# Sums over d of the first layer, moved from VectorE to ScalarE, in a fused interaction network

## The chip, the cores and the metric

One core of one Trainium2 chip runs the whole program. The metric is device microseconds of one execution, as the median of several. Times of instructions come from one profiled execution.

## The reference

For each of 2048 samples, 32 embedding rows of 16 numbers are gathered from 32 tables (x0: sample b, field m, dimension d). Three layers follow, each with 64 outputs k:

    xk = relu(einsum('bmd,bhd,mhk->bkd', x0, xk, W))
    outs.append(sum(xk, axis=d))

The first layer takes xk = x0 (32 rows h), the other two the 64 rows of the layer before. The 3 x 64 sums over d, joined with 16 dense features, go through an MLP of 208 to 512 to 256 to 1 with relu between. Everything is float32.

## The kernel before

**Tiling.** 64 samples make a turn; there are 32 turns (`STEPS`), indexed by s. Sample and d lie along the free dimension (1024 columns, `COLS`), and (m, h) pairs lie along the 128 partitions. A layer is a sum over chunks of 128 such pairs: the products x0[m] * xk[h] are made elementwise, and TensorE contracts them with the weights. Each chunk is contracted in two halves of 512 columns, half b into rows 64b to 64b+63 of a PSUM tile. The first layer (`layer0` in the code) has 5 chunks, since its products are symmetric; `layer1` and `layer2` (the second and third layer) have 16 each.

**Turn s** holds layer1(s) and layer2(s - 1), and in TensorE's queue layer0(s + 1) behind chunk 3 of layer2(s - 1). The MLP of 128 samples is spread over two turns: `mlp1` in even turns, `mlp2` and `mlp3` in odd ones. `mlp3` shares PSUM tile `acc0` with layer0.

**VectorE** makes 15 of the 16 product chunks of each of layer1 and layer2 in groups of 1 to 3 chunks, 7 from `xa` (plain copy of the layer's output, h rows twice) and 8 from `xb` (the same rows turned), both in PSUM. A ring of 10 chunks (`p_dve`) lies between it and TensorE. It also sums over d: `sums(s, n)` is one reduction of a 128 x 512 tile `out_l` into 32 columns per partition of `z`, one for each layer n in each turn. In a steady turn the queue holds: 3 groups of layer1 from xa; `sums(s, 0)`; `sums(s - 2, 1)`; 3 groups of layer1 from xb; `sums(s - 2, 2)`; 3 groups of layer2 from xa; 4 groups of layer2 from xb.

**GpSimd** gathers the table rows by indirect DMAs (16 a turn), makes the first layer's products from `q_tile` and one chunk (`p_pool`) of each other layer.

**ScalarE** evicts PSUM with relu. Its order in turn s is `x1_b(s)` (8 operations), `out_2(s - 2)`, `x2_a(s - 1)` (4 operations, allowed once VectorE is through with the xa groups of layer1(s)), `squares(s + 1)` (the first layer's fifth chunk, which waits for the DMA of `q_tile`), the eviction of mlp1 or mlp2, `x2_b(s - 1)` (8 operations, allowed once VectorE is through with the xb groups of layer1(s), and needed by the xb groups of layer2(s - 1)), mlp3's in odd turns, `x2_s` (the copy for GpSimd), `out_1`, in odd turns the moves of `z` into the MLP's input, then `x1_a(s + 1)`, `x1_s(s + 1)` and `out_0(s + 1)`, which writes the SBUF tile `out_l[:, 0]` that `sums(s + 1, 0)` reads. What is called plain x2 is `x2_a`.

**SyncE** loads the operand tiles (`spread`, `q_tile`) from a scratch tensor in device memory.

Of the kernel before, what the change touches and what calls it, by code (L numbers as in the profile page):

```python
# [7 lines left out]
ACT = mybir.ActivationFunctionType  # L8
# [6 lines left out]
DIM = 16  # L15
# [3 lines left out]
SB = 64  # L19
# [51 lines left out]
def dve_from(s, layer):  # L71


    if layer == 1:
        return max(0, 2 * CD * s - CD)
    return min(2 * CD * (s + 1), 2 * CD * STEPS - CD)
# [10 lines left out]
def build_kernel(nc, ids, table, first_row, dense_t, w0_mh, w0_hm, w1, w2, w_top1, b_top1, w_top2,  # L87
                 b_top2, w_top3, scratch, y):
    with ExitStack() as ctx:
        def sb(name, shape, dt=F32):  # L90
            return ctx.enter_context(nc.sbuf_tensor(name, shape, dt))
# [4 lines left out]
        def sem(name):  # L96
            return ctx.enter_context(nc.semaphore(name))
# [10 lines left out]
        out_l = sb("out_l", [P, 3, BLK])  # L108
        z = sb("z", [P, 2, 3, 2, SB // 2])
# [44 lines left out]
        out_ready = [sem(f"out{n}_ready") for n in range(3)]  # L154
        z_made = [sem(f"z{n}_made") for n in range(3)]
        z_moved = sem("z_moved")
# [146 lines left out]
        def _(act):  # L303
            def relu_a(acc, signal):

                for b in range(2):
                    for to in 0, K:
                        last = nc.scalar.activation(xa[to:to + K, b * BLK:(b + 1) * BLK],  # L308
                                                    acc[b * K:(b + 1) * K, :], ACT.Relu)
                last.then_inc(signal, 1)  # L310

            def relu_b(acc, signal):

                for b in range(2):
                    lo, hi = acc[b * K:b * K + FIELDS, :], acc[b * K + FIELDS:(b + 1) * K, :]
                    for q in range(Q):
                        last = nc.scalar.activation(  # L317
                            xb[q * FIELDS:(q + 1) * FIELDS, b * BLK:(b + 1) * BLK],
                            hi if q % 2 == 0 else lo, ACT.Relu)
                last.then_inc(signal, 1)  # L320
# [9 lines left out]
            def squares(s):  # L330

                act.wait_ge(q_loaded, 16 * Q * (s + 1))
                if s > 0:
                    act.wait_ge(l0_used, C0 * s)
                nc.scalar.activation(p_l0[0:FIELDS, CP, :], q_tile[0:FIELDS, :],  # L335
                                     ACT.Square).then_inc(squares_made, 1)
# [16 lines left out]
            def out_0(s):  # L353
# [2 lines left out]
                    act.wait_ge(z_made[0], s)  # L356
                nc.scalar.activation(out_l[:, 0, :], acc0[:], ACT.Relu).then_inc(out_ready[0], 1)

            def x1_b(s):

                if s == 1:
                    act.wait_ge(dve_made, CD)
                if s >= 2:
                    act.wait_ge(dve_made, dve_from(s - 2, 2) + CD)
                relu_b(acc0, x1b_ready)

            def x2_a(s):

                act.wait_ge(dve_used, dve_from(s, 1) + CD)
                if s + 1 < STEPS:  # L370
                    act.wait_ge(dve_made, dve_from(s + 1, 1) + POOL_CHUNK)
                else:
                    act.wait_ge(dve_made, dve_from(s - 1, 2) + POOL_CHUNK)
                relu_a(acc1[s % 2], x2a_ready)

            def x2_b(s):

                if s + 1 < STEPS:
                    act.wait_ge(dve_made, dve_from(s + 1, 1) + CD)
                else:  # L380
                    act.wait_ge(dve_made, dve_from(s - 1, 2) + CD)
                relu_b(acc1[s % 2], x2b_ready)
# [13 lines left out]
            def out_2(s):  # L396

                act.wait_ge(dve_used, dve_from(s, 2) + CD)
                if s > 0:
                    act.wait_ge(z_made[2], s)  # L400
                nc.scalar.activation(out_l[:, 2, :], acc2[:], ACT.Relu).then_inc(out_ready[2], 1)  # L401
# [24 lines left out]
            def mlp1(t):  # L426

                act.wait_ge(mlp_made, 3 * t + 1)
                for n in range(H1 // P):
                    last = nc.scalar.activation(h1[:, n, :], acc0[:, n * P:(n + 1) * P], ACT.Relu,  # L430
                                                bias=bt1[:, n:n + 1])
                last.then_inc(mlp_done, 1)
                if t + 1 < TILES:
                    load_dense(t + 1)

            def mlp2(t):

                act.wait_ge(mlp_made, 3 * t + 2)
                for n in range(H2 // P):
                    last = nc.scalar.activation(h2[:, n, :], acc0[:, n * P:(n + 1) * P], ACT.Relu,  # L440
                                                bias=bt2[:, n:n + 1])
                last.then_inc(mlp_done, 1)
# [16 lines left out]
            for s in range(STEPS):  # L459
                t = s // 2 - 2  # L460
                even = s % 2 == 0
                x1_b(s)
                if s >= 2:
                    out_2(s - 2)
                if s >= 1:
                    x2_a(s - 1)
                if s + 1 < STEPS:
                    squares(s + 1)
                if t >= 0 and even:
                    mlp1(t)  # L470
                if t >= 0 and not even:
                    mlp2(t)
                if s >= 1:
                    x2_b(s - 1)
                if t >= 0 and not even:
                    mlp3(t)
                if s >= 1:
                    x2_s(s - 1)
                    out_1(s - 1)
                if s % 2 == 1 and s >= 3:  # L480
                    move_z01(s // 2 - 1)
                    move_z2(s // 2 - 1)
                if s + 1 < STEPS:
                    x1_a(s + 1)
                    x1_s(s + 1)
                    out_0(s + 1)
# [17 lines left out]
        def _(dve):  # L504
# [33 lines left out]
            def sums(s, n):  # L538

                if s % 2 == 0 and s >= 4:  # L540
                    dve.wait_ge(z_moved, s // 2 - 1)
                dve.wait_ge(out_ready[n], s + 1)
                nc.vector.reduce_sum(z[:, s // 2 % 2, n, s % 2, :],  # L543
                                     out_l[:, n, :].rearrange("p (i d) -> p i d", d=DIM),
                                     AX_X).then_inc(z_made[n], 1)
# [26 lines left out]
            for s in range(STEPS):  # L572
                for c, n in GROUPS_L1:
                    if c == NT:
                        sums(s, 0)
                        if s >= 2:
                            sums(s - 2, 1)
                    if s == 0 and c == L0_OF_1_AFTER + 1:
                        first_layer_products(1)
                    layer1(s, c, n)  # L580
                if s >= 2:
                    sums(s - 2, 2)
                if s >= 1:
                    for c, n in GROUPS_L2:
                        layer2(s - 1, c, n)
# [178 lines left out]
```

## Time and profile before

| | |
|---|---|
| median of 3 runs | 1191.82 us (1191.45 to 1193.62) |
| profiled execution | 1192.97 us, span 1191.2 us |
| TensorE matmul busy | 1121.3 us (94%) |
| VectorE busy | 1118.8 us (94%) |
| GpSimd busy | 918.8 us (77%) |
| ScalarE busy | 733.9 us (62%) |
| mean granted TensorE clock | 0.991 of full speed |
| a steady turn | 34.62 us |

In rows of the timeline a line is a run of like instructions: start, duration of the whole run, engine, source line, what is written and read, and the count; in square brackets the idle time of the engine ahead of it and what ended it. A float32 matmul leaves two records in the trace, and so does its weight load, so 148 records of the layers are 74 matmuls, one turn's worth. A matmul record's end is modelled, so its pace is read from starts.

### The profile page before, as it was taken

The page shows a single profiled execution, that of the slowest core. Times are in us where ns is not written, and L with a number is a line of the kernel's source. Part 1 is how long each engine was busy: PE and PEld are TensorE (multiplying, and loading weights), DVE is VectorE, ACT ScalarE, POOL GpSimd, SP SyncE. Part 2 cuts the span into 40 slices and gives each one's busy share as a digit, 9 for nine tenths or more (in the row PEclk, how much of TensorE's full clock was granted, in tenths as well). Part 3 has the DMA queues.
Part 4 walks back from the last instruction along what each step waited for, and adds up shares of the span by engine and source line. Part 5 has one row for each costly group of instructions (what it writes and reads, how often), then busy time and mean ns, then how long its engine had stood idle before and what let it go on. Part 6 is the DMA issues. An engine that isn't in the chain of part 4 may idle for free.

```text
span 1191.2 us, 14658 instructions
## 1 busy us (share of the span) xinstructions
PE 1121.3 (94%) x5312; PEld 393.6 (33%) x5312; DVE 1118.8 (94%) x521; ACT 733.9 (62%) x1361; POOL 918.8 (77%) x640
## 2 busy tenths in 40 slices
PE   0488899999999999999999999999999999999997
PEld 0122223333333333333333333333333333333333
DVE  0487999999999999999999999999999999999995
ACT  0343666676667667665766766576676657657653
POOL 6688888888888888888888888888888888885400
PEclk9888999999999999999999999999999999999999
DMA  5887787667678766677876666788666778876300
GB/s 110 190 176 146 158 171 155 138 132 144 140 157 171 157 141 141 132 144 150 172 163 136 143 134 145 144 171 168 139 140 134 143 145 169 166 144 144 61 1 1
DMA packets 76216, 167.25 MB, mean 140 GB/s; under 512 B 21776, under 2 KB 39072, under 8 KB 76144
## 3 DMA queue, kind: packets, MB, share of 16 engines
q1 hardware_dynamic: 59216, 161.95, 64.8%
q0 software_dynamic: 16384, 4.23, 3.6%
q8 instruction: 42, 0.69, 0.3%
q10 hardware_dynamic: 544, 0.14, 0.1%
q14 instruction: 30, 0.25, 0.1%
HBM read 157.86 MB, written 8.40 MB: 140 GB/s over the span
## 4 chain that ended last, share of the span: by engine, by line
PE 86%; POOL 3%; DVE 3%; DMA 3%; issue 3%; ACT 1%; SPq 1%; DVEq 0%
PE acc L600 80%; POOL x_rows L254 3%; DVE p_dve L516 3%; PE acc L672 3%; PE acc L658 1%; PE acc L660 1%; DMA q_tile<-x_of_steps 1%; ACT xb L317 1%; DMA x_rows<-in_table,ids_s 1%; PE acc L680 1%; DMA spread<-x_of_steps 1%; SPq L192 1%; DMA x_of_steps<-x_rows 0%; SPq L219 0%; DVE z L543 0%
## 5 line engine op out<-in xcount | busy, mean ns | idle before, releaser
L600 PE MATMUL acc<-p_dve,w_s 128*64 128x512 f32 x3840 | 863.2, 598 | 22.5 <-DVE p_dve L516 21.8
L254 POOL DMA_INDIRECT x_rows<-in_table,ids_s x512 | 493.7, 964 | 146.1 <-issue 131.2
L516 DVE TENSOR_TENSOR p_dve<-spread,xb 128x3072 f32<-128x3072 f32 (+2 forms) x224 | 572.2, 2682 | 2.9 <-issue 2.9
L516 DVE TENSOR_TENSOR p_dve<-spread,xa 128x2048 f32<-128x2048 f32 (+1 forms) x192 | 501.5, 2730 | 16.6 <-issue 9.1
L600 PEld LDWEIGHTS acc<-p_dve,w_s 128*64 128x64 f32 x3840 | 267.9, 137 | 571.5 <-issue 467.2
L317 ACT ACTIVATE xb<-acc 32x512 f32<-32x512 f32 x512 | 288.8, 564 | 71.6 <-DVE p_dve L516 65.5
L266 POOL TENSOR_TENSOR p_l<-spread,q_tile 128x2048 f32<-128x2048 f32 x60 | 272.7, 4573 | 11.0 <-DMA q_tile<-x_of_steps 10.4
L308 ACT ACTIVATE xa<-acc 64x512 f32<-64x512 f32 x256 | 145.9, 570 | 189.6 <-PE acc L600 155.0
L277 POOL TENSOR_TENSOR p_pool<-spread,x_s 128x1024 f32<-128x1024 f32 x64 | 152.2, 2378 | 94.7 <-PE acc L600 45.9
L600 PE MATMUL acc<-p_l,w_s 128*64 128x512 f32 (+1 forms) x640 | 152.5, 612 | 41.6 <-DVE p_l L556 41.6
L326 ACT ACTIVATE x_s<-acc 64x512 f32<-64x512 f32 x256 | 151.5, 592 | 8.3 <-ACT y_row L449 4.8
L335 ACT ACTIVATE p_l<-q_tile 32x1024 f32<-32x1024 f32 x32 | 33.8, 1057 | 112.8 <-DMA q_tile<-x_of_steps 112.8
L600 PEld LDWEIGHTS acc<-p_l,w_s 128*64 128x64 f32 (+1 forms) x640 | 43.7, 139 | 144.9 <-issue 140.3
L543 DVE TENSOR_REDUCE z<-out_l 128x32 f32<-128x512 f32 x96 | 68.8, 776 | 4.5 <-ACT out_l L401 4.5
L600 PE MATMUL acc<-p_pool,w_s 128*64 128x512 f32 x256 | 65.8, 592 | 0.0
L672 PEld LDWEIGHTS acc<-h,wt 128*128 128x128 f32 x256 | 29.8, 191 | 13.6 <-issue 12.2
L672 PE MATMUL acc<-h,wt 128*128 128x128 f32 x256 | 32.8, 281 | 1.2 <-ACT h L430 1.2
L556 DVE TENSOR_TENSOR p_l<-spread,q_tile 128x2048 f32<-128x2048 f32 x4 | 9.2, 2291 | 25.8 <-DMA spread<-x_of_steps 25.8
L401 ACT ACTIVATE out_l<-acc 128x512 f32<-128x512 f32 x32 | 19.2, 600 | 19.4 <-PE acc L600 19.4
L600 PEld LDWEIGHTS acc<-p_pool,w_s 128*64 128x64 f32 x256 | 18.4, 137 | 36.5 <-issue 36.5
L658 PE MATMUL acc<-z_all,wt 128*128 128x128 f32 x128 | 26.4, 287 | 2.0 <-ACT z_all L407 2.0
L407 ACT ACTIVATE z_all<-z 64x64 f32<-64x64 f32 x96 | 24.3, 253 | 5.3 <-DVE z L543 4.1
(18 smaller groups left out, 151.1 us busy)
## 6 DMA issues: line engine op xcount, KB each, us to landing
spread<-x_of_steps SPq DMA_DIRECT2D x248, 512.0 KB, 17.4
q_tile<-x_of_steps SPq DMA_DIRECT2D x128, 128.0 KB, 11.4
x_rows<-in_table,ids_s POOLq DMA_INDIRECT x512
x_of_steps<-x_rows SPq DMA_DIRECT2D x64, 128.0 KB
spread<-x_of_steps SPq DMA_DIRECT2D x16, 256.0 KB, 5.4
w_s<-in_w SPq DMA_DIRECT2D x2, 512.0 KB, 5.7
wt<-in_w_top SPq DMA_DIRECT2D x1, 512.0 KB, 6.5
z_all<-in_dense_t ACTq DMA_DIRECT2D x16, 8.0 KB, 8.2
```

The lines of the kernel that those rows point to most:

```text
L254: nc.gpsimd.indirect_dma_start(out=x_rows[:, s % 2, i * DIM:(i + 1) * DIM], out_offset=None, in_=table, in_offset=bass.IndirectOffsetOnAxi ...
L266: nc.gpsimd.tensor_tensor(p_l0[:, c:c + 2, :], spread[:, s % 3, c:c + 2, :], q, ALU.mult).then_inc(l0_made, 2)
L277: nc.gpsimd.tensor_tensor(p_pool[:], spread[:, s % 3, POOL_CHUNK, :], x_s[:, layer - 1, :], ALU.mult).then_inc(pool_made, 1)
L308: last = nc.scalar.activation(xa[to:to + K, b * BLK:(b + 1) * BLK], acc[b * K:(b + 1) * K, :], ACT.Relu)
L317: last = nc.scalar.activation(xb[q * FIELDS:(q + 1) * FIELDS, b * BLK:(b + 1) * BLK], hi if q % 2 == 0 else lo, ACT.Relu)
L326: last = nc.scalar.activation(x_s[to:to + K, layer - 1, b * BLK:(b + 1) * BLK], acc[b * K:(b + 1) * K, :], ACT.Relu)
L335: nc.scalar.activation(p_l0[0:FIELDS, CP, :], q_tile[0:FIELDS, :], ACT.Square).then_inc(squares_made, 1)
L516: nc.vector.tensor_tensor(p_dve[:, to:to + n, :], spread[:, s % 3, tile:tile + n, :], over(x[:], n), ALU.mult).then_inc(dve_made, n)
L543: nc.vector.reduce_sum(z[:, s // 2 % 2, n, s % 2, :], out_l[:, n, :].rearrange("p (i d) -> p i d", d=DIM), AX_X).then_inc(z_made[n], 1)
L600: last = nc.tensor.matmul(acc[b * K:(b + 1) * K, :], w, prod[:, b * BLK:(b + 1) * BLK], start=start, stop=stop)
L658: nc.tensor.matmul(acc0[:, cols], wt1[:, 0, cols], z_all[:, 0, :], start=True, stop=False)
L672: last = nc.tensor.matmul(acc0[:, cols], wt2[:, k, cols], h1[:, k, :], start=(k == 0), stop=(k == H1 // P - 1))
```

## The change

`sums(s, 0)`, one VectorE reduction a turn, goes. In its place ScalarE makes the 32 sums of a turn by 32 activations of 128 x 16 columns each, in place on `out_l`, with relu (which changes nothing, since the tile has been through relu) and an accumulator output into one column of `z`. Sixteen of them stand behind `x2_a(s - 1)`, ahead of `squares(s + 1)`; sixteen behind the eviction of mlp1 or mlp2, ahead of `x2_b(s - 1)`. They do this in each turn from 0 on; in turn 0, where no x2_a is, both batches lie around `squares(1)`.

```diff
+            def sums_0(s, part):
+                act.wait_ge(out_ready[0], s + 1)
+                if part == 0 and s % 2 == 0 and s >= 4:
+                    act.wait_ge(z_moved, s // 2 - 1)
+                for i in range(part * SB // 4, (part + 1) * SB // 4):
+                    cols = out_l[:, 0, i * DIM:(i + 1) * DIM]
+                    last = nc.scalar.activation(cols, cols, ACT.Relu,
+                                                accum_out=z[:, s // 2 % 2, 0, s % 2, i:i + 1])
+                if part == 1:
+                    last.then_inc(z_made[0], 1)
...
                 if s >= 1:
                     x2_a(s - 1)
+                sums_0(s, 0)
                 if s + 1 < STEPS:
                     squares(s + 1)
                 if t >= 0 and even:
                     mlp1(t)
                 if t >= 0 and not even:
                     mlp2(t)
+                sums_0(s, 1)
                 if s >= 1:
                     x2_b(s - 1)
...
                     if c == NT:
-                        sums(s, 0)
                         if s >= 2:
                             sums(s - 2, 1)
```

## Rows read from the trace of the kernel before

**Rows 1.** The chain that ended last, two steady turns: start, duration, what.

```profile
548.82 32.38 PE acc L600 x148
581.20 1.98 PE acc L672 x16
583.18 7.02 PE acc L600 x32
590.73 25.34 PE acc L600 x116
618.05 32.39 PE acc L600 x148
```

**Rows 2.** Timeline of VectorE, one steady turn (s odd) and the next start.

```profile
569.99 7.83 DVE L516 TENSOR_TENSOR p_dve<-spread,xa 128x3072 f32<-128x3072 f32 x3
577.65 1.36 DVE L543 TENSOR_REDUCE z<-out_l 128x32 f32<-128x512 f32 x2
578.84 8.89 DVE L516 TENSOR_TENSOR p_dve<-spread,xb 128x3072 f32<-128x3072 f32 x3
587.56 0.77 DVE L543 TENSOR_REDUCE z<-out_l 128x32 f32<-128x512 f32 x1
588.16 7.83 DVE L516 TENSOR_TENSOR p_dve<-spread,xa 128x2048 f32<-128x2048 f32 x3
595.82 8.96 DVE L516 TENSOR_TENSOR p_dve<-spread,xb 128x3072 f32<-128x3072 f32 x4
604.61 7.83 DVE L516 TENSOR_TENSOR p_dve<-spread,xa 128x3072 f32<-128x3072 f32 x3
```

**Rows 3.** Timeline of TensorE's weight loads: steady pace, then a late chunk.

```profile
606.89 0.14 PEld L600 LDWEIGHTS acc<-p_dve,w_s 128*64 128x64 f32 x2 [0.29 <-issue]
...
615.04 0.14 PEld L600 LDWEIGHTS acc<-p_dve,w_s 128*64 128x64 f32 x2 [0.28 <-issue]
...
627.48 0.14 PEld L600 LDWEIGHTS acc<-p_dve,w_s 128*64 128x64 f32 x2 [0.29 <-issue]
628.46 0.20 PEld L600 LDWEIGHTS acc<-p_dve,w_s 128*64 128x64 f32 x4 [0.84 <-DVE p_dve L516]
628.94 0.14 PEld L600 LDWEIGHTS acc<-p_dve,w_s 128*64 128x64 f32 x2 [0.29 <-issue]
```

**Rows 4.** Timeline of ScalarE, the same odd turn.

```profile
577.92 2.31 ACT L308 ACTIVATE xa<-acc 64x512 f32<-64x512 f32 x4 [1.22 <-DVE p_dve L516]
584.64 1.06 ACT L335 ACTIVATE p_l<-q_tile 32x1024 f32<-32x1024 f32 x1 [4.41 <-DMA q_tile<-x_of_steps]
585.73 0.63 ACT L440 ACTIVATE h<-acc,bt 128x128 f32<-128x128 f32 x2
587.77 4.59 ACT L317 ACTIVATE xb<-acc 32x512 f32<-32x512 f32 x8 [1.42 <-DVE p_dve L516]
...
595.41 0.60 ACT L394 ACTIVATE out_l<-acc 128x512 f32<-128x512 f32 x1
595.90 1.57 ACT L407 ACTIVATE z_all<-z 64x64 f32<-64x64 f32 x6
```

**Rows 5.** Timeline of ScalarE, the next even turn: the MLP's four evictions.

```profile
618.92 1.14 ACT L430 ACTIVATE h<-acc,bt 128x128 f32<-128x128 f32 x4
```

**Rows 6.** Groups of instructions by line and form: busy time, mean ns of one.

```profile
L335 ACT ACTIVATE p_l<-q_tile 32x1024 f32<-32x1024 f32 x32 | 33.8, 1057 | 112.8 <-DMA q_tile<-x_of_steps 112.8
L407 ACT ACTIVATE z_all<-z 64x64 f32<-64x64 f32 x96 | 24.3, 253 | 5.3 <-DVE z L543 4.1 <-ACT y_row L449 0.3
L430 ACT ACTIVATE h<-acc,bt 128x128 f32<-128x128 f32 x64 | 18.3, 368 | 6.8 <-PE acc L660 6.4
```

**Rows 7.** Timeline of ScalarE in turn 1.

```profile
85.53 2.31 ACT L308 ACTIVATE xa<-acc 64x512 f32<-64x512 f32 x4 [0.26 <-DVE p_dve L516]
99.53 1.06 ACT L335 ACTIVATE p_l<-q_tile 32x1024 f32<-32x1024 f32 x1 [11.69 <-DMA q_tile<-x_of_steps]
100.61 4.59 ACT L317 ACTIVATE xb<-acc 32x512 f32<-32x512 f32 x8
```

**Rows 8.** Timeline of VectorE from turn 1 to the start of turn 4.

```profile
105.30 8.88 DVE L516 TENSOR_TENSOR p_dve<-spread,xb 128x3072 f32<-128x3072 f32 x4 [2.89 <-issue]
120.06 7.75 DVE L516 TENSOR_TENSOR p_dve<-spread,xa 128x3072 f32<-128x3072 f32 x3 [5.88 <-issue]
...
154.67 7.75 DVE L516 TENSOR_TENSOR p_dve<-spread,xa 128x3072 f32<-128x3072 f32 x3
...
189.28 7.76 DVE L516 TENSOR_TENSOR p_dve<-spread,xa 128x3072 f32<-128x3072 f32 x3
```

**Rows 9.** Timeline of TensorE in the last turn: the one wait for VectorE.

```profile
1153.17 2.79 PE L600 MATMUL acc<-p_dve,w_s 128*64 128x512 f32 x12 [0.70 <-DVE p_dve L516]
```

## The prediction

> **What bounds the kernel now.** I read the busy shares first: TensorE and VectorE are both at 94%, so neither share says which one sets the pace. The chain that ended last is TensorE's matmuls nearly without a break [rows 1]: two turns take 618.05 - 548.82 = 69.23 us. The timeline of VectorE shows, over the same stretch, no idle time at all and a turn of 604.61 - 569.99 = 34.62 us [rows 2], twice which is 69.24. So two engines are full at once, and the question is by how much each would be shorter if the other were not there.
>
> VectorE's own need is its queue as it stands, 34.62 us. TensorE's own need comes from the starts of its weight loads: in a smooth stretch 19 steps take 615.04 - 606.89 = 8.15 us, 0.429 us for one matmul (two records) [rows 3]. Over the two turns I looked for steps that are longer than that, and longer than the same step of the other turn where shapes change. One remains: 628.94 - 627.48 = 1.46 us for six records, where 3 x 0.429 = 1.29 are needed, and it is ended by a product of VectorE [rows 3]. So TensorE loses 0.17 us in two turns; its floor is (69.24 - 0.17) / 2 = 34.53 us a turn, only 0.09 below what VectorE gives it. That is the number on which all depends.
>
> **Removed: one reduction a turn on VectorE.** Two in a row take 578.84 - 577.65 = 1.19 us, a single one 588.16 - 587.56 = 0.60 [rows 2]; so 0.59 us go, and VectorE's own need falls to 34.03 us. With 34.53 of TensorE above it, a steady turn gains 0.09 us and not 0.59. Over the 28 turns from turn 4 on, where MLP work makes TensorE full, that is 2.4 us. In turns 2 and 3 there is no MLP work in TensorE's queue and VectorE alone sets the pace, (189.28 - 120.06) / 2 = 34.61 us [rows 8]: 2 x 0.59 = 1.2 us. In the last turn TensorE waits 0.70 us for VectorE [rows 9], which would then be ahead: 0.7 us. In turns 0 and 1 VectorE waits afterwards for loads or ScalarE, so the reduction there is worth nothing. Sum of gains: 4.3 us.
>
> **Added: 32 small activations a turn on ScalarE.** No row shows one of 16 columns, nor one with an accumulator output. Length: between the SBUF-to-SBUF rows of 1024 columns, 1057 ns, and of 64 columns, 253 ns, a column costs 804 / 960 = 0.84 ns, so one of 16 columns lasts 253 - 40 = 213 ns [rows 6]. Overlap: the four evictions of mlp1, which all start at partition 0, take 1.14 us at a mean of 368 ns, so one starts each (1140 - 368) / 3 = 257 ns, 111 before the end of the last [rows 5, 6]. The four of x2_a, which change their start partition, take 2.31 us and don't overlap [rows 4]; out_1 (0.60 us) and the move behind it, both written at partition 0, start 0.49 apart [rows 4]. The new ones read and write from partition 0 throughout, so I let them overlap: 213 - 111 = 102 ns each. The accumulator's value must also be written out. From below that costs nothing; from above it is an operation of its own with the whole fixed part of one, 213 - 13 = 200 ns; overlapped like the others, about 90. I take 102 + 90, rounded to 0.20 us for a sum, with ends of 0.10 (nothing for the write-out) and 0.43 (0.22 from start to start for the activation and 0.21 for the write-out, none of it overlapped). The middle is nearest to the evictions of mlp1, the only row here of small operations in one place. A turn's 32 cost 6.4 us, between 3.3 and 13.8.
>
> The Trainium skill ("ScalarE: Activation LUTs", What ACT_TABLE_LOAD costs) gives an activation with immediates 186 ns and 0.833 a column, less about 93 of overlap; by that page 32 would be 3.4 us without a write-out. Against this change speaks "VectorE: DVE Perf Modes" (Two Vector instructions with no wait between them), which says of VectorE that an operation with an accumulator output is two instructions; if it holds on ScalarE the higher sums apply. No row here shows either.
>
> **Where they lie.** VectorE's loop through ScalarE in an odd turn: xa groups of layer1, 577.65 - 569.99 = 7.66 us; 0.27 until x2_a; x2_a 2.34; squares 1.09; mlp2's eviction 0.66; x2_b 4.59 and 0.1 to VectorE; the xb groups of layer2, 604.61 - 595.82 = 8.79 [rows 2, 4]. That is 25.5 us, in an even turn 26.0 (mlp1 has 1.17) [rows 5], mean 25.75. A turn can't be shorter than 25.75 + 32t, t the cost of a sum. Against 34.53 that leaves 8.8 us of room: t up to 0.274 us is hidden in steady turns. At t = 0.20 the first batch (3.2 us) fits into the 4.41 us that ScalarE idles for q_tile's DMA ahead of squares [rows 4]. The second moves x2_b: it would end at 585.7 + 0.66 + 3.2 + 4.7 = 594.3, where VectorE with its 0.59 less wants it at about 595.2. Behind it mlp3's eviction, x2_s, out_1, the moves and x1_a follow in 7.6 us, less than the 8.79 of the xb groups. The later squares only feed the last chunk of the next layer0 and the reload of q_tile, both many us off. The new waits are for ScalarE's own earlier work and stand satisfied.
>
> **Where they don't hide: turn 1.** There q_tile lands late, squares runs at 99.53, x2_b at once behind it [rows 7], and VectorE stands idle for it until 105.30; turn 2 then starts only when TensorE has done layer0 from these products, 120.06 [rows 8]. The first batch lies in the 11.69 us of idling [rows 7], the second stands between squares and x2_b: 16 x 0.20 = 3.2 us straight onto the path. In turn 0 both batches end long before x1_a(1) is due.
>
> **Sum.** +3.2 - 1.2 - 2.4 - 0.7 = -1.1 us. The profiled execution at 1192.97 would be 1191.9; it stood 1.15 above the median of 1191.82, so the median becomes 1190.7. For t from 0.10 to 0.27 the sum runs from -2.7 to +0.0, and a little more near the limit, where the 0.09 and the 0.7 are given back: 1189 to 1195.
>
> **Rivals.**
> (a) Slower: the accumulator's write-out costs more, and VectorE waits for x2_b in every turn. The point is t = 0.274. At t = 0.31 (102 ns and a write-out that does not overlap, 0.21) the turn is 25.75 + 9.9 = 35.7, 1.05 over now, in 29 turns +30, and turn 1 adds 5: 1226. At the upper end, 0.43, the turn is 39.5 and the time near 1340. For it: nothing in the trace shows a write-out, and 32 of them multiply any error. Against: ScalarE's same-partition operations overlap here. Chance 0.35.
> (b) Faster: TensorE isn't at its floor, VectorE alone bounds, and 0.59 us are gained in all of 30 turns: 3.2 - 17.7 = -14.5, 1177. For it: VectorE never idles. Against: TensorE's even pace of 0.429 us for 512 columns with no gaps at a granted clock of 1.00. The Trainium skill ("Perfetto Trace Analysis", Identifying the Most-Contended Engine) says that matmul busy time overstates TensorE and that weight-load busy time is the better gauge; that is 33% here, and by it this rival would win. Chance 0.06.
> (c) Cheaper sums: the write-out is free (t = 0.10), turn 1 costs 1.6: 1189.1, just past the bound below. Chance 0.06.
>
> **How the numbers follow.** A measurement of this kernel can tell about 0.2%, 2.4 us, from no change. Forecast, within that: 0.53, with its own range 1189 to 1195. Faster is (b) and (c), 0.12; slower is (a), 0.35. The range of 8 in 10 reaches down to 1187, which leaves out (b), and up to 1226, into (a) as far as t = 0.31, which leaves out the dearer write-outs, some 0.14.
>
> **What would show each step.** VectorE's turn has one reduction behind the xa groups and small idle times for TensorE's ring; TensorE's pace stays 0.429 without the late chunk; its turn is 34.53. Sixteen sums take about 3.2 us ahead of squares, and the wait for q_tile shrinks from 4.4 to about 1.2. In turn 1 VectorE's xb groups of layer2 start at about 108.5. The prediction is wrong if 32 sums take over 8.8 us a turn: then VectorE idles for x2_b and TensorE for VectorE in each turn.

## The result and the profile after

The changed kernel takes 1205.6 us, median of 4 runs (1203.23 to 1209.21), beside 1191.63 us of the kernel before. The ratio is 1.0114, 95% interval [1.0093, 1.0135]: slower, by more than the interval. The forecast was 1190.7, no change. The profiled execution took 1203.23 us with a span of 1201.4 us, against 1192.97 and 1191.2 before. It is the shortest of the four: the traces are 10.2 us apart, the medians 14.0.

The first thing to read is the page: busy shares, the chain's shares, and the groups of ScalarE by line (busy time, mean ns of one, idle time ahead and what ended it).

```profile
PE 1119.5 (93%) x5312; PEld 392.2 (33%) x5312; DVE 1102.0 (92%) x489; ACT 952.2 (79%) x3409; POOL 919.3 (77%) x640
...
PE 76%; ACT 8%; issue 5%; DVE 4%; DMA 3%; POOL 3%; SPq 1%; DVEq 0%; ACTq 0%
...
L367 ACT ACTIVATE out_l<-out_l 128x16 f32<-128x16 f32 x1024 | 205.1, 207 | 42.4 <-issue 41.3
L367 ACT ACTIVATION_READ_ACCUMULATOR out_l<-out_l 128x1 f32 x1024 | 196.8, 193 | 31.4 <-issue 30.9
```

L367 is the line of the sums. Each is two instructions, an activation of 207 ns (forecast: 213) and an accumulator read of 193 ns. The new thing is at the right: 42.4 + 31.4 = 73.8 us of idle time ahead of these instructions, nearly all ended by "issue". ScalarE waited there for no semaphore that the profile shows; the next instruction just was not there. ScalarE now also takes 8% of the chain.

The word "issue" alone would be weak evidence here, for this trace lacks records. Some 8.9 thousand landings of DMAs are in it, against 16.0 thousand in that of the kernel before, so that the page has no time to landing for the operand tiles any more (the line after, then before):

```profile
spread<-x_of_steps SPq DMA_DIRECT2D x248, 512.0 KB
spread<-x_of_steps SPq DMA_DIRECT2D x248, 512.0 KB, 17.4
```

What carries the reading is the program: inside a batch it has no wait at all.

The timeline of ScalarE in an odd turn (start, duration, then what; in brackets idle time ahead), only the ends of the batches and the sums with idle time ahead:

```profile
583.97 2.31 ACT L308 ACTIVATE xa<-acc 64x512 f32<-64x512 f32 x4 [2.09 <-PE acc L614]
586.21 0.20 ACT L367 ACTIVATE out_l<-out_l 128x16 f32<-128x16 f32 x1
586.32 0.19 ACT L367 ACTIVATION_READ_ACCUMULATOR out_l<-out_l 128x1 f32 x1
...
589.02 0.22 ACT L367 ACTIVATE out_l<-out_l 128x16 f32<-128x16 f32 x1 [0.53 <-issue]
...
590.44 0.22 ACT L367 ACTIVATE out_l<-out_l 128x16 f32<-128x16 f32 x1 [0.92 <-issue]
...
591.17 0.22 ACT L367 ACTIVATE out_l<-out_l 128x16 f32<-128x16 f32 x1 [0.22 <-issue]
...
591.88 0.20 ACT L367 ACTIVATION_READ_ACCUMULATOR out_l<-out_l 128x1 f32 x1 [0.50 <-issue]
592.00 1.04 ACT L335 ACTIVATE p_l<-q_tile 32x1024 f32<-32x1024 f32 x1
593.06 0.62 ACT L453 ACTIVATE h<-acc,bt 128x128 f32<-128x128 f32 x2
...
596.87 4.59 ACT L317 ACTIVATE xb<-acc 32x512 f32<-32x512 f32 x8
```

The first batch starts at its forecast pace, one sum (two instructions) in 0.20 us, and then dries up: it lasts 592.00 - 586.21 = 5.79 us, where 3.2 were forecast. The second batch, between 593.58 and 596.87, has no gap (3.27 us). The wait for `q_tile` of [rows 4] is gone altogether. The next even turn is worse:

```profile
618.19 2.31 ACT L308 ACTIVATE xa<-acc 64x512 f32<-64x512 f32 x4 [0.63 <-PE acc L614]
620.53 0.22 ACT L367 ACTIVATE out_l<-out_l 128x16 f32<-128x16 f32 x1
...
627.58 1.06 ACT L335 ACTIVATE p_l<-q_tile 32x1024 f32<-32x1024 f32 x1 [0.51 <-issue]
...
628.67 1.14 ACT L443 ACTIVATE h<-acc,bt 128x128 f32<-128x128 f32 x4
...
632.99 4.59 ACT L317 ACTIVATE xb<-acc 32x512 f32<-32x512 f32 x8
```

627.58 - 620.53 = 7.05 us for the first batch, 3.85 over the forecast. VectorE's timeline shows who pays (`xb` groups of layer2 wait in the program for x2_b):

```profile
576.13 7.75 DVE L531 TENSOR_TENSOR p_dve<-spread,xa 128x3072 f32<-128x3072 f32 x3
583.79 0.68 DVE L558 TENSOR_REDUCE z<-out_l 128x32 f32<-128x512 f32 x1
...
601.56 8.88 DVE L531 TENSOR_TENSOR p_dve<-spread,xb 128x3072 f32<-128x3072 f32 x4
610.35 7.74 DVE L531 TENSOR_TENSOR p_dve<-spread,xa 128x3072 f32<-128x3072 f32 x3
...
637.67 8.88 DVE L531 TENSOR_TENSOR p_dve<-spread,xb 128x3072 f32<-128x3072 f32 x4 [2.00 <-issue]
646.47 5.55 DVE L531 TENSOR_TENSOR p_dve<-spread,xa 128x3072 f32<-128x3072 f32 x2
```

One reduction stands where two stood in [rows 2]. The odd turn takes 610.35 - 576.13 = 34.22 us, the even one 646.47 - 610.35 = 36.12 us, because VectorE idles 2.00 us ahead of the `xb` groups of layer2, for x2_b, which ends at 637.58. Two turns take 70.34 us against 69.24 before; over turns 4 to 30 the mean is 943.87 / 27 x 2 = 69.9, so this pair is a dear one. The chain that ended last, written out in another pair of turns, no longer stays on TensorE:

```profile
376.08 1.98 PE acc L686 x16
378.06 5.33 PE acc L614 x24
383.41 0.68 DVE z L558
384.30 1.91 issue
386.20 3.36 DVE p_dve L531
389.61 1.94 PE acc L614 x8
```

**Where the 10.2 us of span went**, by the starts of turns on VectorE in the two traces (the last row of each step is VectorE's last reduction, 1181.39 before):

| stretch | before | after | difference |
|---|---|---|---|
| start to turn 2 | 120.06 | 121.99 | +1.9 |
| turns 2 and 3 | 69.22 | 68.51 | -0.7 |
| turns 4 to 30 | 934.48 | 943.87 | +9.4 |
| turn 31 to the last reduction | 57.63 | 57.27 | -0.4 |
| last reduction to the end | 9.8 | 9.8 | 0.0 |

### The profile page after: what moved, and what is told of

The parts are those of the page before. It is cut to its first block, busy times and chain, and to the rows that moved or that the text cites. A ratio compares the mean times of both kernels' runs of the same rounds, so it can differ in the third digit from the quotient of the medians.

```text
span 1201.4 us, 16674 instructions
## 1 busy us (share of the span) xinstructions
PE 1119.5 (93%) x5312; PEld 392.2 (33%) x5312; DVE 1102.0 (92%) x489; ACT 952.2 (79%) x3409; POOL 919.3 (77%) x640
## 4 chain that ended last, share of the span: by engine, by line
PE 76%; ACT 8%; issue 5%; DVE 4%; DMA 3%; POOL 3%; SPq 1%; DVEq 0%; ACTq 0%
PE acc L614 71%; DVE p_dve L531 4%; ACT out_l L367 3%; POOL x_rows L254 3%; ACT xb L317 2%; PE acc L686 2%; PE acc L672 1%; DMA x_rows<-in_table,ids_s 1%; PE acc L674 1%; ACT xa L308 1%; DMA q_tile<-x_of_steps 1%; DMA spread<-x_of_steps 1%; SPq L192 1%; ACT p_l L335 1%; DVE z L558 0%
## 5 line engine op out<-in xcount | busy, mean ns | idle before, releaser
L614 PE MATMUL acc<-p_dve,w_s 128*64 128x512 f32 x3840 | 861.4, 598 | 25.4 <-DVE p_dve L531 22.6
L531 DVE TENSOR_TENSOR p_dve<-spread,xb 128x3072 f32<-128x3072 f32 (+2 forms) x224 | 566.3, 2589 | 25.8 <-issue 25.7
L531 DVE TENSOR_TENSOR p_dve<-spread,xa 128x2048 f32<-128x2048 f32 (+1 forms) x192 | 496.0, 2641 | 17.0 <-issue 6.6
L266 POOL TENSOR_TENSOR p_l<-spread,q_tile 128x2048 f32<-128x2048 f32 x60 | 273.2, 4581 | 10.2 <-DMA q_tile<-x_of_steps 7.8
L367 ACT ACTIVATE out_l<-out_l 128x16 f32<-128x16 f32 x1024 | 205.1, 207 | 42.4 <-issue 41.3
L367 ACT ACTIVATION_READ_ACCUMULATOR out_l<-out_l 128x1 f32 x1024 | 196.8, 193 | 31.4 <-issue 30.9
L558 DVE TENSOR_REDUCE z<-out_l 128x32 f32<-128x512 f32 x64 | 43.7, 685 | 4.9 <-ACT out_l L414 4.9
L686 PEld LDWEIGHTS acc<-h,wt 128*128 128x128 f32 x256 | 29.8, 191 | 13.6 <-issue 12.2
L686 PE MATMUL acc<-h,wt 128*128 128x128 f32 x256 | 32.8, 281 | 1.2 <-ACT h L443 1.2
```

What stands on the lines that cost most here:

```text
L266: nc.gpsimd.tensor_tensor(p_l0[:, c:c + 2, :], spread[:, s % 3, c:c + 2, :], q, ALU.mult).then_inc(l0_made, 2)
L367: last = nc.scalar.activation(cols, cols, ACT.Relu, accum_out=z[:, s // 2 % 2, 0, s % 2, i:i + 1])
L531: nc.vector.tensor_tensor(p_dve[:, to:to + n, :], spread[:, s % 3, tile:tile + n, :], over(x[:], n), ALU.mult).then_inc(dve_made, n)
L558: nc.vector.reduce_sum(z[:, s // 2 % 2, n, s % 2, :], out_l[:, n, :].rearrange("p (i d) -> p i d", d=DIM), AX_X).then_inc(z_made[n], 1)
L614: last = nc.tensor.matmul(acc[b * K:(b + 1) * K, :], w, prod[:, b * BLK:(b + 1) * BLK], start=start, stop=stop)
L686: last = nc.tensor.matmul(acc0[:, cols], wt2[:, k, cols], h1[:, k, :], start=(k == 0), stop=(k == H1 // P - 1))
```

## Experiments

The theory after the result: TensorE still has its floor, and 16 sums cost what was forecast; what pushes the even turns over is that ScalarE's small instructions come late in the first batch. The rivals: TensorE had no such floor; the sums themselves are dearer beside other work; the gathers of GpSimd make the instructions late (in the trace of the result all batches with gaps have gathers beside them, and those without gathers, the second ones from turn 1 on and all of the last two turns, have no gaps).

**Without the sums.** Both calls of the batches and the reduction are left out; `z` of the first layer is set once, so those MLP inputs are not the reference's.

```diff
-                sums_0(s, 0)
...
-                sums_0(s, 1)
```

> Leaves out the first layer's sums over d: neither VectorE nor ScalarE makes them (z of that layer is set once to a constant), all else as in the changed kernel. Both theories on ScalarE expect the whole gain of the prediction without its cost: 1191.8 - 4.3 = 1187.5 us, a steady turn of 34.53 us set by TensorE at 0.429 us for one matmul. If TensorE is not at its floor (rival b), 0.59 us in each of 30 turns goes: about 1175 us.

1189.19 us (ratio 0.9979, [0.9965, 0.9993]). VectorE's timeline:

```profile
598.88 7.75 DVE L515 TENSOR_TENSOR p_dve<-spread,xa 128x3072 f32<-128x3072 f32 x3 [0.32 <-PE acc L600]
...
633.06 7.75 DVE L515 TENSOR_TENSOR p_dve<-spread,xa 128x3072 f32<-128x3072 f32 x3
```

This turn takes 34.18 us, the one before it 34.88, together 69.06: twice the 34.53 that [rows 3] gave. VectorE has 0.59 us a turn less to do and now idles for TensorE (the 0.32 and like gaps). So the floor of TensorE is real, rival (b) falls, and cheaper sums could bring about what this run shows, 1191.71 - 1189.19 = 2.5 us. It is no sharp bound: a kernel further down that does make the sums took 1187.51, and the end of the run alone moves a time by 2.6 us (last table).

**Same length in longer instructions, and the same instructions without accumulator.** In the first, each batch is 12 activations of 180 columns into a spare tile; in the second the 16 activations stand but have no accumulator output. Both leave the first layer's sums out.

```diff
-                for i in range(part * SB // 4, (part + 1) * SB // 4):
...
+                for i in range(LONG):
...
+                    nc.scalar.activation(filler[:, n % 2], out_l[:, 0, 0:FILL],
+                                         ACT.Relu).then_inc(filled, 1)
```

> The 32 sums are replaced by few long activations at the same places (12 a batch, of 180 columns, 24 a turn, without accumulator output), which keep ScalarE's engine about as long: 12 x (0.094 + 0.151) = 2.9 us against 3.2 for 16 sums. Leaves out the first layer's sums. Theory A (the engine time of the sums is as forecast, and what costs is that ScalarE runs out of instructions inside the first batch): no idle time inside the batches, steady pair of turns 69.1 us, turn 1 pays 2.9: about 1190.5 us. Rival (ScalarE's added busy time is itself too long for the room ahead of x2_b): even turns stay at 35.5 to 36 us, 1200 us or more.

1193.12 us (ratio 1.0004, [0.9990, 1.0018]): 12 instructions of 345 ns in a batch have no gaps, two turns take 69.06, and only turn 1 pays. This fits theory A, but it can't decide for it: the changed kernel itself had no gaps when it ran on this chip later.

```diff
-                    last = nc.scalar.activation(cols, cols, ACT.Relu,
-                                                accum_out=z[:, s // 2 % 2, 0, s % 2, i:i + 1])
+                    last = nc.scalar.activation(cols, cols, ACT.Relu)
```

> The 32 small activations stay where they are, but without accumulator output, so 16 instructions a batch and not 32; leaves out the first layer's sums. Theory A (the first 20 to 24 small instructions come at once, those behind them late while GpSimd issues gathers): no idle time inside either batch, 1.6 us a batch, a pair of turns 69.1, about 1189.5 us. Rival (late instructions by time since the batch began, or from the first one on): idle time inside the first batch remains.

1191.68 us (ratio 0.9992, [0.9980, 1.0004]). Groups of ScalarE by line in this kernel:

```profile
L368 ACT ACTIVATE out_l<-out_l 128x16 f32<-128x16 f32 x1024 | 114.4, 206 | 0.4
```

1024 activations keep ScalarE busy for 114.4 us when nothing stands between them, 0.112 each from start to start: the forecast's 0.102 for the activation. With the read between them a sum is 0.20, so the read adds about 0.09.

**Without the gathers.** From turn 4 on small GpSimd operations stand in their place and the table rows are a constant, so the output is not the reference's.

```diff
+                if s >= 4:
+                    nc.gpsimd.tensor_tensor(filler[:], ...)
+                    nc.gpsimd.memset(x_rows[:, s % 2, i * DIM:(i + 1) * DIM], 0.05).then_inc(set_rows[s % 2], 1)
+                    return
                 nc.gpsimd.indirect_dma_start(
```

> The changed kernel, but from turn 4's rows on GpSimd makes no gathers: in place of each indirect DMA one product of 360 columns and one small memset of the rows, of about the gather's length; the embedding rows are therefore constants. Theory A1 (ScalarE's instructions come late while GpSimd issues indirect DMAs): the idle time inside the first batch is gone from then on, 16 sums take 3.2 us in every turn, steady pair of turns near 69.1, about 1191 us. Rival A2 (about 22 small instructions in a row is all that ScalarE can be given, whatever GpSimd does): the idle time of about 2.3 us a turn stays, 1203 to 1206 us.

1193.75 us (ratio 1.0018, [1.0007, 1.0028]), no gap, two turns 69.06. It looked like proof for the gathers, but it was run in another comparison than the result, and on a chip on which the changed kernel, gathers and all, later ran without gaps too (the fourth chip below). So it proves nothing of them.

**One batch only, and the second batch elsewhere.** In the first, ScalarE makes the second 16 sums and VectorE the first 16 (a reduction of half the tile). In the second kernel the second batch stands behind x2_b.

```diff
-                sums_0(s, 0)
...
+                        half_sums(s)
```

> Only the second batch is on ScalarE; the first 16 of the 32 sums stay on VectorE as one reduction of 128 x 256 (about 0.33 us). Theory A: the second batch has no idle time and fits into the room, a pair of turns 69.1; turn 1 pays 3.2: 1191.8 - 0.5 - 2.4 - 0.7 + 3.2 = 1191.4 us. Rival (each batch costs by its own length, in proportion): half of the loss of the whole change, 1198 us.

1190.62 us (ratio 0.9990, [0.9981, 0.9999]); turns of 34.36 and 34.70, together 69.06.

```diff
-                sums_0(s, 1)
                 if s >= 1:
                     x2_b(s - 1)
                 if t >= 0 and not even:
                     mlp3(t)
+                sums_0(s, 1)
```

> All sums stay on ScalarE; the second batch moves behind x2_b and mlp3's eviction, ahead of x2_s, where ScalarE used to idle 3.0 to 4.9 us for TensorE. Theory A (what costs is the way to x2_b: 25.5 or 26.0 us, 6.4 for 32 sums, 2.6 or 3.4 for late instructions in the first batch): the way shrinks by 3.2 to 31.3 and 32.5 us, under TensorE's 34.53, late instructions or not; turn 1 no longer pays either: 1187.5 to 1189.5 us, a pair of turns 69.1. Rival (ScalarE's total work or later steps such as x1_a and x2_s now bind): pairs of turns stay near 70, 1200 us or more.

1189.56 us (ratio 0.9979, [0.9968, 0.9990]). Two turns are 69.06 here too, and turn 2 starts at 116.53 (119.33 to 120.02 in three later traces of this kernel): in turn 1 x2_b no longer waits for sixteen sums. But this trace has no gaps in its first batch either, which stands where it stood in the result, beside gathers.

**From turn 2 on.** VectorE makes the sums of turns 0 and 1, ScalarE the others.

```diff
             def sums_0(s, part):
+                if s < 2:
+                    return
...
+                        if s < 2:
+                            sums(s, 0)
```

> The changed kernel, but in turns 0 and 1 VectorE makes the sums as before. The start-up term of the prediction alone: 3.2 us less than the changed kernel's 1205.6, so 1202.4 us. If the batch in turn 1 is hidden after all, 1205.6.

1187.51 us (ratio 0.9965, [0.9956, 0.9975]), some 15 us under what was expected from the result: again no gap, although all of its steady turns are those of the changed kernel. The expectation's other half held roughly: turn 2 starts at 119.51, 2.5 us before the 121.99 of the result, where 3.2 were expected. At this point every kernel but the result's ran without gaps, edited or not in the place that mattered. The open question was no longer which part of the change, but whether the changed kernel itself does it again.

**The changed kernel again, on other chips.** No edit; a first time, beside two others, alone, and as a gauge for two more.

> The changed kernel itself, once more and on the chip of this comparison. The variants with the sums in the same or other places showed no late instructions on ScalarE, also where the batch lies beside gathers. If the late instructions belong to this program (its batches in turns 0 and 1, or where its instructions lie), they are here again: idle time of 2 to 3 us a turn in the first batch, 1203 to 1208 us. If they belonged to the chip or the load of that first run, they are gone: a pair of turns 69.1, turn 1 pays 3.2, 1190 to 1193 us.

> The changed kernel, now on one chip with the next two. Theory P (late instructions belong to the program): 1203 to 1209 us here, with idle time inside its first batches, while the next two stay at 1187 to 1190. Theory C (they belong to the chip on which a kernel runs; c1 ran on another chip than the variants): all three of this call show them or none does. With none, this is 1190 to 1193 us: 0.25 less than 1191.8 for two turns of start-up paying 3.2.

> The changed kernel once more. It took 1205.6 and 1207.9 us in two comparisons where it was the only kernel beside the one before, and 1193.4 us on a chip where two others were loaded too. If the chip decides, the time here is either near 1193 or near 1207 us with the records of its semaphores complete or lacking as they were there; if being the only other kernel decides, it is near 1207 us on whatever chip.

> The changed kernel as it is, again, as the gauge of the chip for the two kernels run behind it. If this chip is like those of the result and of its first repeat, ScalarE's first batch shows idle times of 0.2 to 0.9 us between its small operations beside GpSimd's gathers, odd and even turns together take about 70.1 us, and the ratio is 1.011 to 1.013. If it is like the others, the batch runs at 0.10 us an operation without a gap, two turns take 69.06, and the ratio is 1.000 to 1.001.

| run of the changed kernel | us | ratio to before | gaps in the batches |
|---|---|---|---|
| the result | 1205.6 | 1.0114 [1.0093, 1.0135] | 73.8 us |
| again, second chip | 1207.92 | 1.0131 [1.0110, 1.0152] | 77.0 us |
| again, third chip | 1193.42 | 1.0011 [1.0002, 1.0021] | none |
| again alone, fourth chip | 1192.87 | 1.0002 [0.9990, 1.0013] | none |
| again, fifth chip | 1193.49 | 1.0008 [0.9998, 1.0017] | none |

The kernel before took 1191.6 to 1192.6 us in all five comparisons. The number of the result's chip is not on record; the other four are four chips. The groups of ScalarE by line, on the second chip and then on the fifth:

```profile
L367 ACT ACTIVATE out_l<-out_l 128x16 f32<-128x16 f32 x1024 | 205.1, 207 | 35.5 <-issue 34.8
L367 ACT ACTIVATION_READ_ACCUMULATOR out_l<-out_l 128x1 f32 x1024 | 197.1, 194 | 41.5 <-issue 40.7
```

```profile
L367 ACT ACTIVATE out_l<-out_l 128x16 f32<-128x16 f32 x1024 | 203.8, 207 | 0.4
L367 ACT ACTIVATION_READ_ACCUMULATOR out_l<-out_l 128x1 f32 x1024 | 196.8, 193 | 0.0
```

Same program, same mean duration, 77 us of idle time or 0.4. And all executions of one comparison are of one kind: 1202.8 to 1211.3 us in the two with gaps, 1188.7 to 1195.2 in the three without. So the +1.1% does not come of the program alone. It goes with the chip or with a state in which a comparison ran; the changed kernel met each chip once, so the runs can't tell these apart. It is not a matter of what ran beside it: the fourth chip ran it alone, without gaps.

One more thing parts the two kinds, and it is a rival that no run tests. The second chip's trace lacks landings just as the result's does, 8.9 thousand against 16.0 thousand in every trace without gaps whose kernel makes all its gathers. They are lacking where the gaps are: in the first batches of turns 2 to 29 the result's trace has 3.4 landings recorded per us and the fifth chip's 23.6; in the second batches, which have no gaps, 19.5 and 18.9. Every time of this case is that of a recorded execution, with its span and its clock. So it may be the recording itself that holds ScalarE up on those two occasions, and the loss may not be there without it. On the fifth chip the first batch, which has no gap, also runs beside gathers; the timeline of ScalarE and that of GpSimd:

```profile
579.63 0.20 ACT L367 ACTIVATE out_l<-out_l 128x16 f32<-128x16 f32 x1
...
584.94 1.06 ACT L335 ACTIVATE p_l<-q_tile 32x1024 f32<-32x1024 f32 x1 [2.04 <-DMA q_tile<-x_of_steps]
```

```profile
579.33 0.94 POOL L254 DMA_INDIRECT x_rows<-in_table,ids_s  x1 [0.30 <-issue]
580.58 0.95 POOL L254 DMA_INDIRECT x_rows<-in_table,ids_s  x1 [0.30 <-issue]
581.83 0.95 POOL L254 DMA_INDIRECT x_rows<-in_table,ids_s  x1 [0.30 <-issue]
```

The batch takes 584.94 - 2.04 - 579.63 = 3.27 us and the wait for `q_tile` is 2.04. Gathers alone don't make the instructions late; on a chip that has the lateness they may be what it takes.

**Both batches in one place**, ahead of x2_b behind the eviction.

```diff
-                sums_0(s, 0)
...
+                sums_0(s, 0)
                 sums_0(s, 1)
```

> All 32 sums stand behind the MLP's eviction, ahead of x2_b, where GpSimd is inside its 9 us products and issues no gathers. Theory A1: no idle time in the run of 64 small instructions in steady turns, 6.4 us; ScalarE's loop is 25.8 + 6.4 = 32.2 us, under TensorE's 34.53; turn 1 pays 6.4 us instead of 3.2: 1191.8 - 4.3 + 6.4 = 1193.9 us. Rival A2: of 64 instructions in a row the last 40 come at the slow pace of 0.35 us each instead of 0.1, 10 us more in each turn: over 1300 us, and at least 1220.

1216.46 us (ratio 1.0222, [1.0190, 1.0254]), 22.6 us over theory A1, and this is no matter of late instructions: 64 in a row take 6.45 us without a gap (on a chip, though, where the changed kernel had none either). ScalarE has the same work, and in steady turns 31 to 33 us of it on the way to x2_b as before. What changed is what the first batch overlaps: it used to run while squares waited for `q_tile`, and now it stands behind squares, so from `q_tile`'s landing to x2_b it is 3.2 us more. VectorE waits for x2_b, and GpSimd for x2_s behind it; the timelines of both:

```profile
609.21 8.88 DVE L531 TENSOR_TENSOR p_dve<-spread,xb 128x3072 f32<-128x3072 f32 x4 [1.70 <-issue]
```

```profile
597.25 9.10 POOL L266 TENSOR_TENSOR p_l<-spread,q_tile 128x2048 f32<-128x2048 f32 x2
...
612.23 2.37 POOL L277 TENSOR_TENSOR p_pool<-spread,x_s 128x1024 f32<-128x1024 f32 x1 [0.99 <-ACT x_s L326]
...
621.33 2.38 POOL L277 TENSOR_TENSOR p_pool<-spread,x_s 128x1024 f32<-128x1024 f32 x1 [1.86 <-PE acc L614]
```

The rows suggest a loop over two turns: GpSimd's products of the first layer 9.1, 4 gathers 5, the last one's landing and the store 3.9, SyncE's issues 3.7, `q_tile`'s DMA 11.3, squares 1.06, the evictions of mlp2 and mlp3 1.2, 32 sums 6.45, x2_b 4.7, x2_s 2.4, and on GpSimd two products and 12 gathers, 19.8: 68.6 us, and 70.5 with GpSimd's wait of 1.86, against 69.06. With one batch ahead of squares it is 3.2 less and hidden. Two turns take 953.48 / 27 x 2 = 70.6 us on average here (turns 4 to 30). This reading of the loop is from the rows; no run took one member of it away.

**The two better orders again**, three of the four with the changed kernel in the same comparison (e11 without it).

> The variant whose sums move to ScalarE from turn 2 on, again, beside the changed kernel. Theory P: 1187.5 us, no idle time in its batches. Theory C: like the changed kernel, with idle time in the first batches and 1200 us or more if this chip is of that kind; 3 us below the changed kernel in either case.

> The variant with the second batch behind x2_b, again, beside the changed kernel. Theory P: 1189.5 us. Theory C on a chip with late instructions: the way to x2_b has 3.2 us less, so that they are hidden: 1190 us all the same, with idle time in its batches.

> The variant with the second batch behind x2_b, once more, to meet a chip with late instructions. There, with 2.6 to 3.4 us of idle time in the first batch, the way to x2_b is 31.3 and 32.5 us, under 34.53: 1189 to 1191 us with the idle time visible. On a chip without: 1189 us, no idle time.

> Second batch behind x2_b instead of ahead of it. Only if the changed kernel shows the idle times on this chip does this run tell something new: then the late first batch costs 3.3 + 2.6 to 3.4 us ahead of squares, the way to x2_b is 25.5 or 26.0 + 3.2 + 3.4 = 32.1 to 32.6 us, under TensorE's 34.53, two turns take 69.06 and the ratio is 0.997 to 0.998. The rival, that late instructions cost time wherever the sums stand (through GpSimd's loop), gives two turns of 70 us and more and a ratio over 1.008. On a chip without idle times both give 0.997 to 0.998.

From turn 2 on: 1188.89 us (0.9968, [0.9957, 0.9980]). Behind x2_b: 1188.64 (0.9971, [0.9957, 0.9985]), 1189.13 (0.9971, [0.9950, 0.9992]) and 1189.47 (0.9973, [0.9962, 0.9983]), on three chips. On the first and the last of these the changed kernel took 1193.42 and 1193.49. Both orders so beat the changed kernel, by what is saved in turn 1 (on the fifth chip the order behind x2_b starts turn 2 at 120.02 and not at 122.78), and the kernel before, by the shorter turns after it. None of these four traces has a gap in its first batch, though, and so nothing is shown for a chip with late instructions. Two more runs left the gathers out, with the changed kernel or the order behind x2_b beside them:

> The changed kernel without gathers from turn 4 on (rows are constants), once more, to meet a chip with late instructions. If the gathers make them late there: idle time in the batches of turns 0 to 2 only, about 1194 us. If not: idle time of 2 to 3 us in the first batch of each turn, 1203 us or more. On a chip without: 1193.8 us.

> The changed kernel with the gathers of turn 4 and later left out (small operations of about the same length stand in their place on GpSimd, so the table rows are not the reference's). Again it tells something only if the changed kernel shows the idle times on this chip: if the gathers beside the batch make ScalarE's instructions late, the idle times go and two turns take 69.06 us, ratio 1.000 to 1.002; if something else of the chip does it, they stay, two turns take 70.1 and the ratio is 1.011 to 1.013.

1193.62 us (1.0008, [0.9997, 1.0020]) and 1192.80 (0.9998, [0.9986, 1.0009]), no gaps, on chips where the kernel beside them had none either. The gathers' share stays unsettled.

## Why the prediction was wrong

**The failed step** is "A turn can't be shorter than 25.75 + 32t", with t = 0.20 wherever the sums stand. It prices the instructions and assumes that they are there when the engine is free. In the comparisons without gaps it holds; in the result's trace the first batch costs 5.79 us in an odd turn and 7.05 in an even one instead of 3.2. With the second batch at 3.27 the way of VectorE through ScalarE in the even turn is 36.12 us from start to start, 3.85 of it lateness. Without that it would be 32.27, and 2.26 us of room would be left under 34.53; the lateness is 1.59 more than the room. The odd turn's way is 34.22, just under. Together 1.59 - 0.31 = 1.28 over 69.06, the measured 70.34. The odd turn could give back little more than these 0.31, because VectorE's own need there is 34.03. The outcome is that of rival (a), VectorE waits for x2_b, by another mechanism: its point, t = 0.274, was never reached by the price of a sum.

**The price of a sum held.** 0.102 for the activation, 0.09 for the write-out were taken; 0.112 and about 0.09 were measured, 3.27 us for 16. Of the bounds, 0.10 would have asked for a free write-out and 0.43 for no overlap; neither is so.

**The floor of TensorE held**, 69.06 us in two turns in all kernels without gaps but the one with both batches in one place. It rested on one late chunk of 0.17 us, and it decided that removing 0.59 us from VectorE is worth 0.09.

**Where nothing is late, the sum can be read term by term**, here from the fifth chip's trace of the changed kernel against that of before:

| term | forecast | measured |
|---|---|---|
| turn 1, second batch on the path | +3.2 | +2.7 (turn 2 starts at 122.78 and not 120.06) |
| turns 2 and 3 | -1.2 | -1.2 (190.84 - 122.78 = 68.06) |
| turns 4 to 30 | -2.4 | -3.3 (turn 31 starts at 1121.97; 931.13 us) |
| the last turns | -0.7 | -0.4 (last reduction at 1179.24) |
| behind the last reduction | 0 | +2.6 |
| sum | -1.1 | +0.4 |

The xb groups of layer2 in turn 1 start at 108.07, forecast 108.5. One trace gives the first term roughly only: in the three traces of the changed kernel without gaps turn 2 starts at 120.67, 122.78 and 122.85. The one term that no step of the sum had is the last. There the last MLP runs alone on TensorE, and its clock falls to the lower level, 1.2 GHz. The windows of the changed kernel on the fifth chip (stretch, its length, then busy times of PE, PEld, DVE, ACT and POOL with counts, granted clock, DMA share, GB/s), and the 16 matmuls of mlp2 in the timelines of TensorE of this kernel and of the kernel before:

```profile
1178.00:1181.00 3.00, 1.03 (x8) 0.47 (x5) 0.69 (x1) 1.11 (x3) 0.00 (x0) 1.00 0.00 0
1181.00:1184.00 3.00, 2.50 (x15) 2.21 (x13) 0.00 (x0) 0.46 (x2) 0.00 (x0) 0.58 0.00 0
1184.00:1187.00 3.00, 2.26 (x10) 2.26 (x11) 0.00 (x0) 0.69 (x3) 0.00 (x0) 0.50 0.00 0
```

```profile
1184.74 3.73 PE L686 MATMUL acc<-h,wt 128*128 128x128 f32 x16 [1.23 <-ACT h L443]
```

```profile
1185.97 2.05 PE L672 MATMUL acc<-h,wt 128*128 128x128 f32 x16 [1.23 <-ACT h L430]
```

Two clock levels, 2.05 or 3.73 us for the same work, and from the last reduction to the end 9.8 or 12.4 us. Ahead of the last mlp1 TensorE had idled 1.97 us for ScalarE's moves of `z` in both, so this wait does not part them. In the 20 traces of this case the slow end (12.2 to 13.4 us) is there in 12, among the changed kernel's in 3 of 5 (not in the result's); it comes and goes for like kernels. It explains how a kernel that is 2.2 us ahead of before at its last reduction ends 0.4 behind it.

**The range and the chances.** The range, 1187 to 1226, held the result because rival (a) had stretched it, which is luck and not insight. For its price of +34 to +148 (1226 and 1340) was made for a constant dearer sum; what came was a lateness of 2.6 and 3.9 us in the two turns shown against a room of 2.3, and the median rose by 14.0 only. A rival "the instructions don't arrive in time" was not in the list. Nothing in the trace of before bore on it: there ScalarE has some 42 instructions a turn, the shortest of 253 ns [rows 6], and the change adds 64 of about 200.

The Trainium skill ("VectorE: DVE Perf Modes", Two Vector instructions with no wait between them) had said of VectorE that an accumulator output makes two instructions; the 1024 reads of 193 ns agree, for ScalarE. The Trainium skill ("Perfetto Trace Analysis", Identifying the Most-Contended Engine) calls matmul busy time no good measure and judges TensorE's headroom by MFU, the share of peak arithmetic, and by weight-load busy time. The latter is 33% here and would speak for headroom; the run without the sums disagrees, for TensorE is at its floor there with 33%. The Trainium skill ("Runtime: NRT & Kernel Launch", Instruction fetch mechanics) says that a long straight program streams in, its fetch being mostly hidden. The trace of the result has an engine that idles for its next instruction and nothing else; whether the fetch is what is late there, no run shows. The trace speaks against it: the instruction queues moved 42 and 45 packets in the whole span, as on the fifth chip, and none of them starts within the two gapped batches shown (586.21 to 592.00 and 620.53 to 627.58).

**What stays open**: what makes the small instructions late in two of the five comparisons, the chip, the gathers, or the recording, whose records are lacking in the same two. In the result's trace the gaps lie in batches beside gathers alone, but all three runs without gathers fell on chips where no trace has such gaps. Nor was it tried beside such lateness whether the order with the second batch behind x2_b hides it. By the rows it should, since the way to x2_b would be 36.12 - 3.30 = 32.8 us, under 34.53; that is argued and not shown.

## What to carry to other kernels

When an engine gets many instructions of 0.1 us, price not only the instructions but also their arrival: in two of five comparisons a row of 32 came on time for its first 20 to 27 and lasted 2.2 to 4.0 us longer than its work. Measure on more than one chip before believing a loss or a gain of one per cent. By the rows some microseconds of room behind such a row would hide the lateness; that, and whether fewer and longer instructions are spared it, no run shows, for the 12 of 345 ns (3.0 us a batch) ran only where the short ones were on time too. Ask of a batch what stands behind it on its engine: the same sixteen sums behind x2_b cost nothing in turn 1 (turn 2 starts at 116.5 to 120.0, before at 120.06) and leave the kernel 0.3% faster than before; in front of it they cost 0.6 to 2.8 us there. And when two engines are full at once, find the floor of each before counting what taking work off one of them is worth.

## What was unexpected of the hardware

- The same program on ScalarE ran with 0.4 us of gaps in three comparisons and with 74 to 77 us of gaps in two, where a first batch lasts 5.5 to 7.3 us instead of 3.27 (turns 2 to 29). There the first 20 to 27 instructions come at 0.10 us each and then about four in every 1.42 us (590.44 - 589.02). The two traces with gaps are also the two in which over 40% of the landing records are missing.
- The accumulator read of ScalarE is an instruction of 193 ns, and overlaps with its neighbours: activation and read together take 0.20 us from start to start.
- TensorE's clock at the very end of the run, where it waits for other engines, stood at either level from run to run: the stretch behind the last reduction takes 9.8 us or 12.2 to 13.4.
